# The last query tile's two tail stages taken in turn, row block by row block, on one PSUM bank

## What is computed

```python
c_kv = h @ W_dkv + b_dkv                      # 128 wide
c_q  = h @ W_dq  + b_dq
# k, q: 48 columns per head from c_kv / c_q, 16 rotary ones from h / c_q
scores = einsum('bqhd,bkhd->bhqk', q, k) / sqrt(64)
out = einsum('bhqk,bkhd->bqhd', softmax(scores), v).reshape(b, s, 1024) @ W_o + b_o

x = layernorm(h + out)                        # called x1 below
w = simulate_quantize_int4(kernel)
x = layernorm(x + x @ w + bias + (x @ a) @ b)
```

## Time and profile before

| | us |
|---|---|
| median of 3 runs | 3169.63 |
| lowest, highest of them | 3160.61, 3214.21 |
| the profiled execution, its own time | 3162.22 |
| span of its slowest core (core 2) | 3160.7 |
| PE busy | 2490.7 (79%) |
| ACT busy | 2193.9 (69%) |
| DVE busy | 1149.7 (36%) |

### The profile page before, as it was taken

The page is one execution under the profiler, slowest core; times in us unless marked ns, Lnnn a source line. Parts: engine busy times, 40 slices in busy tenths (PEclk is TensorE's granted clock), DMA queues, the critical chain, the costliest instruction groups (busy, mean ns, idle before and its releaser), DMA issues.

```text
span 3160.7 us, 40044 instructions; the slowest of 8 cores (3142.8 to 3160.7 us)
## 1 busy us (share of the span) xinstructions
PE 2490.7 (79%) x10450; PEld 787.4 (25%) x10584; DVE 1149.7 (36%) x1482; ACT 2193.9 (69%) x2481; POOL 230.8 (7%) x393
## 2 busy tenths in 40 slices
PE   3455659999888978898889888897898788988733
PEld 1222312222222222222222222222222222222211
DVE  1356222123343243324432434244323443334244
ACT  1233349999678967897679867985788678977700
POOL 4000000000000000000000000000000000010000
PEclk8566669999899989999899999998999899999966
DMA  6422230001212121202120122012121212121121
GB/s 114 111 93 85 75 75 26 19 20 52 70 36 72 38 86 39 71 29 71 54 75 28 49 74 77 30 46 82 46 61 42 70 49 63 34 79 56 53 93 40
DMA packets 89939, 188.44 MB, mean 60 GB/s; under 512 B 20579, under 2 KB 50532, under 8 KB 89476
## 3 DMA queue, kind: packets, MB, share of 16 engines
q1 hardware_dynamic: 44292, 82.81, 9.4%
q0 software_dynamic: 31616, 77.88, 8.5%
q10 hardware_dynamic: 13824, 25.17, 2.1%
HBM read 144.65 MB, written 51.64 MB: 62 GB/s over the span
## 4 chain that ended last, share of the span: by engine, by line
PE 55%; DVE 14%; ACT 11%; issue 10%; DMA 8%; POOL 1%; SPq 1%; DVEq 0%; ACTq 0%; POOLq 0%; another core or an unknown queue 0%
PE PS L237 53%; ACT Psb L249 5%; DVE tA L254 3%; DVE bcast_sb L280 3%; ACT bcast_sb L249 2%; PE PS L243 2%; ACT wkr_sb L249 2%; DVE h L254 1%; DMA rotq_scr<-c0s_sb 1%; DMA x_scr<-tA 1%; DVE Psb L260 1%; DMA h<-x_scr 1%; DVE x1T L254 1%; DMA h<-h 1%; POOL Vsb L284 1%
## 5 line engine op out<-in xcount | busy, mean ns | idle before, releaser
L249 ACT ACTIVATE Psb<-PS 128x1024 bf16<-128x1024 f32 x1536 | 1518.3, 1042 | 364.5 <-PE PS L237 355.0
L237 PE MATMUL PS<-Psb,Vsb 128*65 128x512 bf16 x3072 | 1002.6, 410 | 111.8 <-ACT bcast_sb L249 98.1
L237 PE MATMUL PS<-Qsb,Ksb 64*128 64x512 bf16 x4096 | 831.3, 399 | 94.4 <-ACT Psb L249 63.4
L249 ACT ACTIVATE wkr_sb<-PS 128x1024 bf16<-128x1024 f32 x512 | 534.3, 1044 | 106.3 <-PE PS L237 102.9
L237 PEld LDWEIGHTS PS<-Qsb,Ksb 64*128 64x128 bf16 x4096 | 221.4, 93 | 955.1 <-issue 952.1
L237 PEld LDWEIGHTS PS<-Psb,Vsb 128*65 128x65 bf16 x3072 | 221.3, 112 | 487.6 <-issue 487.6
L237 PE MATMUL PS<-wkr_sb,Vsb 128*65 128x512 bf16 x1024 | 328.7, 404 | 2.6 <-ACT wkr_sb L249 2.6
L280 DVE RECIPROCAL bcast_sb<-bcast_sb 128x512 f32<-128x512 f32 x64 | 214.4, 3350 | 253.2 <-DMA bcast_sb<-rden 253.1
L254 DVE TENSOR_TENSOR tA<-PS,h 128x512 f32<-128x512 f32 x128 | 88.4, 691 | 557.3 <-PE PS L237 520.7
L276 DVE CAST oun_sb<-PS 64x512 bf16<-64x512 f32 x128 | 87.3, 682 | 425.9 <-PE PS L237 423.8
L237 PE MATMUL PS<-wbuf,osb 128*128 128x512 bf16 x448 | 148.1, 416 | 72.5 <-DVE tA L254 53.6
(11 more groups left out here) (88 smaller groups left out, 1356.2 us busy)
## 6 DMA issues: line engine op xcount, KB each, us to landing
h<-h SPq DMA_DIRECT2D x64, 512.0 KB, 3.9
wbuf<-wo_p POOLq DMA_DIRECT2D x32, 512.0 KB, 6.1
bcast_sb<-rden POOLq DMA_DIRECT2D x128, 128.0 KB, 2.8
x_scr<-tA POOLq DMA_DIRECT2D x32, 512.0 KB, 2.9
wbuf<-wf_p POOLq DMA_DIRECT2D x32, 512.0 KB, 5.6
h<-x_scr SPq DMA_DIRECT2D x32, 512.0 KB, 4.0
out<-tA ACTq DMA_DIRECT2D x32, 512.0 KB, 2.6
o_dram<-oun_sb ACTq DMA_DIRECT2D x64, 128.0 KB, 1.7
```

The lines of the kernel that those rows point to most:

```text
L237: e.matmul(o, l, r, start=s1, stop=s2, tile_position=t, skip_group_check=k)),
L249: e.activation(o, i, f, scale=sc, bias=b)),
```

## The change

`last_qt` becomes true for the last query tile, so that its tail takes the path described above, and this path's T2 is placed on PSUM bank 7 (column 3584, `bank7_free`), the same bank that T1 uses, where the text before named bank 6 (column 3072, `bank6_free`). Nothing changes for the other seven tiles.

```diff
@@ -849,7 +849,7 @@
             st = tail_state
             BK7 = PS[:, 3584:4096]
             x1w_s = [0, 0, 0, 0]
-            last_qt = False
+            last_qt = qt == NQT - 1
             bb = dma("gpsimd", bbuf[:, :], dr["b_o"].partition_broadcast(128),
                      sem="qBB", waits=[("sDV", st["bbuf_free"])]
                      if st["bbuf_free"] else [("sDV", ckv_free)])
@@ -893,8 +893,8 @@
                           sem="qBB", waits=[("sPE", denb[NGT - 1]),
                                             ("qBB", st["bo_ld"])])
                 st["bank6_free"] = qb_state["qb_bank_free"]
-                ctxL = dict(base=3072, tA=tA2, cells=cells2, bbuf=bbuf2,
-                            bfld=bb2["qBB"], tAq="tA_q2", bkfree="bank6_free",
+                ctxL = dict(base=3584, tA=tA2, cells=cells2, bbuf=bbuf2,
+                            bfld=bb2["qBB"], tAq="tA_q2", bkfree="bank7_free",
                             wf=lambda cp_, c, half: (
                                 Ksb[:, 2048 * cp_ + 1024 * (c % 2) + 512 * half:
                                     2048 * cp_ + 1024 * (c % 2) + 512 * (half + 1)],
```

## The result

The changed kernel takes 3201.55 us (median of 10 runs) against 3161.52 for the kernel before (10 runs beside it). The ratio is 1.0113, with a 95% interval of 1.0096 to 1.013: slower by 36 us, within 2%; the two medians are 40 us apart. The forecast was 3193, with 3177 to 3215 around it. In a few executions of either kernel four cores ran at a granted clock of about 0.8 instead of 0.88 (3315.21 and 3337.31 us for the changed one), and the ratios leave these out.

What follows compares the result with a forecast made beforehand. No engine bounds the tail: it is one dependent chain. Terms 23.5 + 1.5 + 2.5 + 0.5 - 1 + 0.5 = +27.5 us on 3162.2 gave 3189.7, moved halfway up to the median: 3193, range 3177 to 3215.

Steps and rivals of the forecast that it cites:

- The round trip of x1: Last tile's tail: four bare waits for x1's write, reload and first transposes, 8.6 us a block; +23.5 us net.
- the second load: Tail, on SP: h's load for the next T1 runs beside x1's reload three times, 0.5 us each, +1.5 us.
- The tail in all: From the first T1 add to the last LayerNorm piece: 147.1 us before, about 172 us forecast after.
- open bound: Tail: a clock raised sooner by earlier activity could save up to 5.8 us in all; not taken into the sum.
- The weight loads during attention: Last attention stretch: four FFN weight loads on POOL's queue delay the denominators' broadcast read and ACT; +2.5 us (1.3 to 7).
- +0.5, -1, +0.5 beside it: PE longer at low clock after the wait, +0.5; T1 matmuls leaving attention, -1; one more DMA for b_ffn, +0.5.
- T1's matmuls leaving the attention: 6 of T1's first 8 matmuls run after the last V matmul, in PE's idle time; -1 us, at most 2.3 back.
- Bank 7 for bank 6: Tail: T1 and T2 never overlap on PE, so sharing the bank costs nothing; without LayerNorm cover 1.9 us a block.
- The choked queue: Rival, last attention stretch: weight loads delay the read some 38 us, slower by over 2%; needs 14.8 us a load; chance 0.04.
- the cheap case: Round trip cheaper than its rows: quick loads, clock rising sooner (-5.8 and -2), attention terms 0; +16 us, about 3182.
- The filled round trip: Rival, tail: next block's T1 fills x1's round trip, -7 to -11 us, about 3158; chance 0.05.
- The expected signs: Timeline: T1 adds 42.7 us apart, four 8 us DVE idles, no tA wait, late broadcast read, ACT waiting 3-9 us, tail 172.

## Why the prediction was right, point by point

**The round trip of x1, +23.5 on the path.** Right in kind and nearly in size. Forecast 8.6 us a block and 0.5 for the second load; found 9.15, 9.19, 9.33 and 8.86. On core 7 the load took 3.96 to 4.18 us with h's load behind it and 3.71 in block 3, where there is none: +0.3 to 0.5, as taken. PE began 0.35 us behind the landing, not 0.13. The experiment with x1 in SBUF took the round trips out and with them the growth. The estimate by the Trainium skill's "DMA: Bandwidth & Descriptors" (anatomy of one DMA), 3.2 us for 512 KB, would have been too short by 0.5 us or more for each load; the page gives its sum for DMAs issued from gpsimd, and these are issued from SP. For x1's write, issued from POOL, it is 0.3 us too long (2.92 us). The trace decides.

**The tail in all, forecast 147.1 + 23.5 + 1.5 = 172.1; found 177.45.** Of the 5.3 us too few, 2.15 are the base: the profiled core 2 had 147.1, at the low end of the 8 cores, whose median is 149.25 (T1's second half takes 3.57 us on six of them, 3.31 on core 2). The round trips, 36.5 in all against 4 x 8.6 + 1.5 = 35.9, are 0.6. Most of the rest is the clock, and there the sum was wrong in sign for its open bound: I kept up to 5.8 us of gain for a clock that rises sooner, and it rose later. On core 7 the FFN matmuls of T2's first half take 3.57 us in every block, where the same core before had 3.57, 3.22, 3.12 and 3.08, and the single matmul behind them 0.60, where it had 0.38 or 0.39 from block 1 on. T2's second half is at the low level in 8 of 32 cases (8 cores, 4 blocks), against 4 of 32 before. (T2's first transposes in the earlier trace rows stand 8 us ahead of their copy, not 9; the sum does not use it.)

**The weight loads during attention, taken at +2.5 with 1.3 to 7, and +0.5, -1, +0.5 beside it; found +5.9.** The mechanism was right, to the order of the DMAs on POOL and the wait of ACT; the term was under-sized. Part of that is the base: core 2, which I read, had the longest such stretch of the 8 cores before, 62.95 us against the median of 61.4, and its wait of 1.85 us, from which I took that there was no slack, stood on one other core only. Against core 2 the growth is 4.4 us. The broadcast read came 1.6 us later and took 1.5 longer, together 3.1, inside the range. Two more things were missed. On core 7, PE stayed at the low level for 6 us instead of some 3 after the wait (taken as +0.5). And T1's matmuls leaving the attention, taken at -1, gave nothing to see: with the loads out of the way the stretch is 61.35 us, against 61.4.

**Bank 7 for bank 6, nothing.** Right: 176.5 against 177.45 us in the tail, whose cores overlap.

**The rivals.** The choked queue would have needed 14.8 us a load; the second load, which waits for the first, was issued 6.7 us behind it on core 7 and 8.1 us on core 2. (The rival's "at 15 it is over 3233" is 3229.5 by its own sum: 3193 - 2.5 + 39; and the terms of the cheap case add up to +17, not +16. Neither decides anything here.) The filled round trip did not come by itself, as one generator writes T1 behind T2; mixed by hand, work overlapped, but the round trip stayed bare until x1 was kept in SBUF. The expected signs were all found, the tail at 177 for 172 and ACT's wait of 4.0 to 6.2 us within the 3 to 9 given.

**The time.** The sum of +27.5 was 8 us short of the measured 36 (30 to 41 by the interval), the range of +16 to +45 held it. That 3193 lies only 8.6 below the median of 3201.55, which is 40 us above that of the kernel before, is in part luck: the base was put 4 us too high, and that goes against the short sum.

## What to carry to other kernels

A second buffer removes a wait only if something else can run in the freed time: ask what the in-order lists of the engines put there. Alternating two stages block by block with a DRAM round trip between them cost four bare round trips here, while running each stage over all blocks hid the reloads; mixing the stages piece by piece and keeping the intermediate in SBUF beat both (tail 114.4 us, against 177.45 and 149.25). And loads that were moved earlier into a queue, each waiting for the one before, delayed the small transfers behind them in it: 6.25 us from the denominators' write to the read, against 2.64 without them.

## What the runs showed that I had not expected

- The granted clock took back part of a shorter wait: with x1 kept in SBUF, PE's idle time ahead of T2 fell from 17.2 us (core 7, changed kernel) to 9.6 (core 6), and yet T2's second half was at the low level 21 times of 32, with early and with late weight loads, in place of 8. The cause is left open; no run here varied it by itself.
- POOL waits 3.1 to 3.6 us for the denominators' write of the last pair but one on the 8 cores of the kernel before, against 1.6 us for that of the last pair. With the weight loads behind the attention and T1's matmuls out of it, it is 1.64 there too (core 0), and the short waits of ACT vanish. What slowed it before was not tried.
